# Second norm of the feed-forward part: VectorE's small operations placed between large ones, three of sixteen pairs scaled on VectorE, the output centred on GpSimd

## The reference

```python
x = _layernorm(x + self_attention(x))            # 16 heads, causal
x = _layernorm(x + cross_attention(x, ctx))      # 8 heads, rotary
h = silu(bitlinear158(x, w1, b1))                # 256 -> 1024
h = gelu(h, exact)
h = layer_norm(h, ln_g, ln_b)                    # over 1024: the second norm's input
y = bitlinear158(h, w2, b2)                      # rms_norm, rounding to 8 bits, 1024 -> 256
x = _layernorm(x + y)
```

## Time and profile before

| | us |
|---|---|
| median of 3 runs | 543.01 (540.65 to 547.83) |
| the profiled execution | 539.41 |
| its span, first to last instruction | 537.3 |
| busy in the span: PE, DVE, ACT, POOL | 428.1, 442.1, 374.3, 287.1 |

### The profile page before, as it was taken

The page is one execution under the profiler, slowest core; times in us unless marked ns, Lnnn a source line. Parts: engine busy times, 40 slices in busy tenths (PEclk is TensorE's granted clock), DMA queues, the critical chain, the costliest instruction groups (busy, mean ns, idle before and its releaser), DMA issues. The chain is left out here.

```text
span 537.3 us, 11851 instructions
## 1 busy us (share of the span) xinstructions
PE 428.1 (80%) x4098; PEld 231.1 (43%) x4098; DVE 442.1 (82%) x948; ACT 374.3 (70%) x700; POOL 287.1 (53%) x390
## 2 busy tenths in 40 slices
PE   6567799999999999999999999998876602555553
PEld 5354445445454554545545555443332201333332
DVE  3755787989889889799998998988749959999993
ACT  2232266678687786777877867677778778999983
POOL 5841646475474655645557446450124547767653
PEclk9676799999999999999999999999998855555557
DMA  6125326442332322323223232221000000000001
GB/s 226 46 77 182 93 57 187 113 114 69 82 96 63 113 70 67 108 52 111 71 64 112 66 95 69 61 89 42 3 0 1 1 0 1 11 30 20 31 30 40
DMA packets 51674, 37.07 MB, mean 69 GB/s; under 512 B 21408, under 2 KB 47648, under 8 KB 51488
## 3 DMA queue, kind: packets, MB, share of 16 engines
q1 hardware_dynamic: 51328, 36.10, 22.9%
q10 hardware_dynamic: 288, 0.23, 0.2%
HBM read 24.52 MB, written 10.49 MB: 65 GB/s over the span
## 5 line engine op out<-in xcount | busy, mean ns | idle before, releaser
L971 DVE TENSOR_REDUCE MX<-mx_b 128x2 f32<-128x512 f32 x256 | 167.1, 679 | 26.5 <-PE mx_b L581 25.4
L780 ACT ACTIVATE PB<-e_b 128x512 f32<-128x512 f32 x256 | 148.1, 592 | 55.2 <-PE e_b L609 54.0
L581 PE MATMUL mx_b<-KA,QA 48*128 48x256 bf16 x512 | 97.6, 275 | 11.5 <-DVE MX L971 10.8
L609 PE MATMUL e_b<-QA,KA 50*128 50x256 bf16 x512 | 97.1, 274 | 1.0 <-DMA QA<-MR 0.7
L626 PE MATMUL u_b<-PB,VA 128*32 128x256 f32 x1024 | 84.0, 391 | 2.0 <-ACT PB L780 1.5
L898 POOL TENSOR_TENSOR SP<-SP,srec 128x1024 f32<-128x1024 f32 x15 | 28.5, 1901 | 79.1 <-DVE srec L943 79.1
L581 PEld LDWEIGHTS mx_b<-KA,QA 48*128 48x128 bf16 x512 | 29.6, 94 | 86.7 <-issue 47.1
L1301 PE MATMUL r_b<-identh,Q 128*128 128x128 f16 x128 | 16.2, 305 | 39.5 <-ACT Q L1214 39.5
L1246 POOL TENSOR_TENSOR H<-H,row_tab 128x1024 f32<-128x1024 f32 x15 | 35.4, 2363 | 21.4 <-ACT H L1204 17.9
L1307 PE MATMUL z_b<-w2q,Q2T 128*128 128x256 bf16 x128 | 28.5, 400 | 19.3 <-ACT Q2T L1225 19.3
L888 POOL TENSOR_TENSOR KM<-QK,att_tab 128x512 f32<-128x512 f32 x31 | 32.0, 1052 | 21.4 <-ACT QK L734 21.4
(11 more groups left out here) (172 smaller groups left out, 1017.0 us busy)
## 6 DMA issues: line engine op xcount, KB each, us to landing
KA<-parts_k SPq DMA_DIRECT2D x64, 96.0 KB
QA<-parts_q SPq DMA_DIRECT2D x64, 96.0 KB
parts_q<-part_q SPq DMA_DIRECT2D x32, 128.0 KB, 1.9
parts_k<-part_k SPq DMA_DIRECT2D x16, 192.0 KB, 2.1
C<-in_ctx SPq DMA_DIRECT2D x16, 128.0 KB, 3.1
X<-in_x SPq DMA_DIRECT2D x16, 128.0 KB, 2.9
out_y<-O SPq DMA_DIRECT2D x16, 128.0 KB, 1.7
XT<-in_xT SPq DMA_DIRECT2D x15, 128.0 KB, 2.2
```

The source lines that it names most:

```text
L581: m = nc.tensor.matmul(mx_b[n % 2][:, D * k:D * k + D], QA[low:low + K_MAX, 2 * i.ring + b, h, P * u:P * u + P], KA[low:low + K_MAX, 2 * i ...
L609: m = nc.tensor.matmul(e_b[n % 2][:, D * k:D * k + D], KA[low:low + K_EXP, 2 * i.ring + b, h, P * sc:P * sc + P], QA[low:low + K_EXP, 2 * ...
L780: nc.scalar.activation(PB[:, n % 4].rearrange("p e t -> p (e t)"), e_b[n % 2][:, :], ACT.Exp, scale=XC ** -0.5).then_inc(e_sb.sem, 1)
L971: nc.vector.tensor_reduce(MX[:, b, e, 2 * q:2 * q + 2, u], mx_b[n % 2][:, :].rearrange("p (e s) -> p e s", e=2), AXL.X, ALU.max).then_inc( ...
```

## The change

- The lags are counted in VectorE's turns now (statistics 0, and so on to the output at 7), 22 turns in all. ScalarE takes gelu one pair ahead, in the same order as before.
- `shift_z` and nmz are gone: GpSimd computes O as (Z - mean) times 1/std, and waits for its own power.
- VectorE's order in a turn: base_n now stands between the shift and the inverse; the multiplier stands between the two halves of the statistics, the divisor behind them. In the first turn in which a pair gets ln_b (t == LAG_Y), this addition stands behind the statistics and not first.
- Pairs 3, 7 and 11 (VEC) are scaled on VectorE, ahead of the factors of the turn, and not on ScalarE.
- GpSimd takes the power over only as many columns as are in use in the first turns. In the drain it takes the rms's power ahead of ln_g, and writes an output in the turn of its sum.
- In turn END (19) VectorE computes the factors of the last two pairs in one turn, ScalarE rounds the last pair one turn earlier, and TensorE transposes it ahead of the product of the pair before.

```diff
@@ -1178,12 +1178,22 @@
             return Pair(0, t - lag) if 0 <= t - lag < NPAIR else None
 
 
-        LAG_G, LAG_N, LAG_Z = 1, 5, 7
+        LAG_G, LAG_Y, LAG_N, LAG_Z = 0, 3, 4, 6
         BASES = list(itertools.accumulate(sum(pair_at(t, lag) is not None for lag in (LAG_G, LAG_N, LAG_Z))
                                           for t in range(TURNS2)))
 
-        DRAIN = NPAIR + LAG_G + 1
+        DRAIN = NPAIR + LAG_G
         ROOTS = list(itertools.accumulate(1 if t < DRAIN else 2 for t in range(TURNS2)))
+        END = TURNS2 - 3
+
+        VEC = (3, 7, 11)
+        zs_vec = sem("zs_vec")
+
+        def wait_scaled(eng, i):
+            if i.v in VEC:
+                eng.wait_ge(zs_vec, sum(v <= i.v for v in VEC))
+            else:
+                eng.wait_ge(zs.sem, i.v + 1 - sum(v <= i.v for v in VEC))
 
         @block.scalar
...
             def second_values(t):
-                if i := pair_at(t, 3):
-                    wait(act, shift, i, 1)
-                    nc.scalar.activation(H[:, i.v, :], H[:, i.v, :], ACT.Identity, bias=nmh[:, i.p, 0:1],
-                                         scale=root[:, (i.v + LAG_G) % 4, 0:1]).then_inc(zs.sem, 1)
-                if i := pair_at(t, 0):
...
-                                         ACT.Identity, bias=nrnd16[:]).then_inc(q2_sb.sem, 1)
+                if t == 0:
+                    gelu_h(Pair(0, 0))
+                if (i := pair_at(t, 2)) and i.v not in VEC:
+                    scale_h(i)
+                if i := pair_at(t, -1):
+                    gelu_h(i)
+                if (j := pair_at(t, 5)) and t <= END:
+                    round_y(j)
+                if i := pair_at(t, LAG_Y):
+                    square_y(i)
+                if t == END:
+                    round_y(last)
+                if j := pair_at(t, 5):
+                    q2t_copy(j)
...
+            def power(t, col, n):
+                nc.gpsimd.tensor_tensor(root[:, t % 4, col:col + n], base[:, t % 2, col:col + n], halves[:, 0:n],
+                                        ALU.pow).then_inc(s_root, 1)
+
+            def row_product(t):
+                if i := pair_at(t, LAG_Y):
+
+                    wait(pool, yn, i, 1)
+                if (i := pair_at(t, 2)) and i.v != NPAIR - 1:
+                    wait_scaled(pool, i)
+                    nc.gpsimd.tensor_tensor(H[:, i.v, :], H[:, i.v, :], gam, ALU.mult).then_inc(zg.sem, 1)
+
+            def output(z, t):
+                pool.wait_ge(s_root, ROOTS[t])
+                if has(z, 2):
+                    pool.wait_ge(st_o[z.p], 16 * z.uses)
+                nc.gpsimd.tensor_scalar(O[:, z.p, :], Z[:, z.ring, :], mvz[:, z.p, 0:1], root[:, t % 4, 2:3],
+                                        ALU.subtract, ALU.mult).then_inc(on.sem, 1)
+
             def turn(t):
-                if i := pair_at(t, 4):
...
-                                                    ALU.pow).then_inc(s_root, 1)
-                        else:
-                            pool.sem_inc(s_root, 1)
-                elif BASES[t] > (BASES[t - 1] if t else 0):
+                if t < DRAIN:
+                    row_product(t)
+                    if z := pair_at(t, LAG_Z + 1):
+                        output(z, t - 1)
                     pool.wait_ge(s_base, BASES[t] + 1)
-                    nc.gpsimd.tensor_tensor(root[:, t % 4, :], base[:, t % 2, :], halves[:, 0:3], ALU.pow).then_inc(s_root, 1)
+                    power(t, 0, 1 + sum(t >= lag for lag in (LAG_N, LAG_Z)))
                 else:
-                    pool.sem_inc(s_root, 1)
+                    if pair_at(t, LAG_N):
+                        pool.wait_ge(s_base, BASES[t - 1] + 2)
+                        power(t, 1, 1)
+                    else:
+                        pool.sem_inc(s_root, 1)
+                    row_product(t)
+                    if t == DRAIN:
+                        output(pair_at(t, LAG_Z + 1), t - 1)
+                    pool.wait_ge(s_base, BASES[t] + 1)
+                    power(t, 2, 1)
+                    output(pair_at(t, LAG_Z), t)
 
             mean_power(pool, 1)
             rstd(pool, ln2, last, mv2, rs2)
...
@@ -1316,6 +1358,10 @@
                     x_out_proj(pe, last, g_b[1])
                 first_product(t)
             for n in range(NPAIR):
+                if n < NPAIR - 1:
+                    q2_transpose(Pair(0, n))
+                if n == NPAIR - 2:
+                    q2_transpose(last)
                 second_product(Pair(0, n))
 
...
+                    wait_scaled(dve, j)
...
+            def base_free(t):
+                if t >= 2:
+                    dve.wait_ge(s_root, ROOTS[t - 2])
 
...
+            def scale_h(i):
+                nc.vector.tensor_scalar(H[:, i.v, :], H[:, i.v, :], mvh[:, i.p, 0:1], root[:, (i.v + LAG_G) % 4, 0:1],
+                                        ALU.subtract, ALU.mult).then_inc(zs_vec, 1)
+
...
+                if has(z, 2):
+                    wait(dve, on, z.plus(-2), 1)
...
+            def y_factors(f, t):
+                prev = root[:, t % 4, :]
+                row_ceiling(f, prev)
+                row_inverse(f)
+                row_multiplier(f, prev)
+                row_divisor(f)
+
             def turn(t):
-                i, j, z = pair_at(t, LAG_G), pair_at(t, 4), pair_at(t, LAG_Z)
-                if j:
+
+                i, j, z = pair_at(t, LAG_G), pair_at(t, LAG_Y), pair_at(t, LAG_Z)
+                f, g, prev = pair_at(t, LAG_N + 1), pair_at(t, LAG_G + 1), root[:, (t - 1) % 4, :]
+                if j and t > LAG_Y:
                     row_added(j)
-                if t > LAG_G:
+                if g:
                     dve.wait_ge(s_root, ROOTS[t - 1])
-                f, g, o = pair_at(t, LAG_N + 1), pair_at(t, LAG_G + 1), pair_at(t, LAG_Z + 1)
-                prev = root[:, (t - 1) % 4, :]
+                if (n := pair_at(t, 2)) and n.v in VEC:
+                    scale_h(n)
...
                     shift_h(g, prev)
+                if s := pair_at(t, LAG_N):
+                    base_n(s, t)
...
                 if f:
-                    row_factors(f, prev)
-                if s := pair_at(t, LAG_N):
-                    base_n(s, t)
-                if i:
-                    wait(dve, gelu, i, 1)
-                    for c in range(2):
-                        nc.vector.bn_stats(sth[:, i.p, 6 * c:6 * c + 6], H[:, i.v, 512 * c:512 * c + 512]).then_inc(hn.sem, 1)
+                    row_multiplier(f, prev)
+                h_stats(i, 1)
+                if f:
+                    row_divisor(f)
+                if j and t == LAG_Y:
...
+                    row_added(j)
                 if z:
                     z_sum(z)
-                if i:
-                    wait(dve, hn, i, 2)
-                    nc.vector.bn_aggr(mvh[:, i.p, :], sth[:, i.p, :]).then_inc(hn.sem, 1)
+                h_mean(i)
                 if z:
                     z_stats(z)
-                if i:
...
+                if j := pair_at(t, LAG_Y):
                     row_added(j)
...
+                    dve.wait_ge(s_root, ROOTS[t - 1])
+                    shift_h(g, root[:, (t - 1) % 4, :])
+                if (f := pair_at(t, LAG_N + 1)) and t <= END:
+                    dve.wait_ge(s_root, ROOTS[t - 1] - int(t > DRAIN))
+                    y_factors(f, t - 1)
                 if s := pair_at(t, LAG_N):
                     base_n(s, t)
                 if j:
                     row_max_abs(j)
...
-                    z_sum(z)
-                    z_stats(z)
-                    z_base(z, t)
+                if t == END:
+                    dve.wait_ge(s_root, ROOTS[t] - 1)
+                    y_factors(last, t)
+                z = pair_at(t, LAG_Z)
+                z_sum(z)
+                z_stats(z)
+                z_base(z, t)
 
             nc.vector.memset(base[:], 1.0).then_inc(s_base, 1)
```

More of the change, by code:

```diff
@@ new lines, in scale_h, with gelu_h, round_y @@
+            def scale_h(i):
+                wait(act, shift, i, 1)
+                nc.scalar.activation(H[:, i.v, :], H[:, i.v, :], ACT.Identity, bias=nmh[:, i.p, 0:1],
+                                     scale=root[:, (i.v + LAG_G) % 4, 0:1]).then_inc(zs.sem, 1)
+            def gelu_h(i):
+                wait(act, silu, i, 1)
+                nc.scalar.activation(H[:, i.v, :], H[:, i.v, :], ACT.Gelu).then_inc(gelu.sem, 1)
+            def round_y(j):
+                wait(act, fac, j, 3)
+                if has(j, 2):
+                    wait(act, q2_ps, j.plus(-2), 1)
+                nc.scalar.activation(Q2[:, j.p, :], H[:, j.v, :], ACT.Identity, bias=rnd16[:],
+                                     scale=sc[:, j.v, 6:7]).then_inc(qd.sem, 1)
@@ new lines, in square_y, with q2t_copy @@
+            def square_y(i):
+                wait(act, yn, i, 1)
+                if has(i, 1):
+                    wait(act, sqr, i.plus(-1), 1)
```

(28 more changed lines are left out.)

75 lines of the change are left out of this document (11 added, 64 removed).

## The result

| | before | after |
|---|---|---|
| median of the runs, us | 541.94 (4 runs, one more than shown above) | 548.92 (4 runs, 547.98 to 549.24) |
| ratio | | 1.0121, 95% interval 1.0068 to 1.0174 |
| profiled execution, its span | 539.41, 537.3 | 549.14, 547.4 |
| first gelu starts, last output ends | 432.3, 534.8 | 436.3, 544.9 |
| the stage between them | 102.5 | 108.5 |

What follows compares the result with a forecast made beforehand. VectorE was taken as the bound. Late addition +1.0, first scaling +0.4, wait for Z +0.4, eight turns +0.6 and drain -1.8 gave +0.6, +0.7 by the last output: 543.7 us, range 538.5 to 547.5.

Steps and rivals of the forecast that it cites:

- nmz between power and output falls away: GpSimd at the drain's end, behind the last rounding: without nmz the output follows the power sooner, -0.4 us.
- stands behind the output of pair 12 and ends near 527.4: GpSimd's power in turn 19 of the drain; the last rounding then starts at 528.1, before at 527.67.
- Full turns: VectorE's turn falls by nmz's 0.12 us to 5.34; ScalarE's stays 5.45; three scalings add 2.0 us.
- turn 15: Turn opened by VectorE's addition at 503.06 before; forecast to start at 505.5, after +1.0, +0.4, +0.4 and +0.6.
- Drain: From turn 15 to the last output: 30.0 us instead of 31.8, -1.8; bounds -3 to -1.
- the prediction's own signs: Wrong if ordinary turns fall much over 0.12, pairs 0 and 1 add no later, or drain gains under 1 or over 3 us.
- Scaling: 128x1024 scaling on VectorE in turns 5, 9 and 13: busy 0.75 us, cost 0.66 each, bounds 0.43 to 1.22.
- Late addition in turn 3: Pair 0's addition behind shift and statistics starts at 442.55 instead of 441.24; the second addition comes 1.0 us later.
- ScalarE waiting "about 1 us": Sign for turns 9 and 13: ScalarE's rounding waits for the multiplier, so its relief of 1.13 us is not used.
- Spreading the factors: VectorE's small operations keep their distances; spreading only avoids inverse and multiplier waiting for their own input, no gain beyond.
- faster rival: ScalarE is the true bound; each scaling gives back 1.13 us, 3.4 in all: 538.8 us, chance 0.27.
- slower rival: Scalings run at the additions' rate and meet GpSimd's power, turns 5, 9, 13: +4.7 to 547.7 us, chance 0.20.

Runs made afterwards that it cites:

- e1: Changed kernel with GpSimd's output as multiply, add instead of subtract, multiply (values not the output's): stage 104.10 us, ratio 1.0011 to the kernel before.
- e2: Changed kernel with GpSimd's output as add, multiply instead of subtract, multiply (values not the output's): stage 103.37 us, one run, 547.32 us.
- e9: Changed kernel with output adding a negated mean, no VectorE scalings, turn 3's addition first, multiplier and divisor directly behind inverse and base: stage 101.98 us, ratio 0.9943.
- e5: e2's kernel with no pair scaled on VectorE (values not the output's): stage 102.10 us, ratio 0.9984 to the kernel before.
- e10: e9 with pairs 6 and 11 scaled on VectorE behind the factors: stage 102.79 us, ratio 1.0015 to the kernel before.
- e12: Changed kernel with no scaling on VectorE and turn 3's addition first, output still subtract, multiply: stage 104.90 us, ratio 0.9992 to the kernel before.
- e13: Changed kernel with GpSimd's power ahead of the output in full turns, drain order as changed: stage 106.26 us, ratio 1.0079 to the kernel before.
- e3: Changed kernel with the output in two GpSimd steps, a one-column nmz, then multiply, add: stage 105.06 us, ratio 1.0016 to the kernel before.
- e4: Kernel before with nmz and shift_z taken out and the output as subtract, multiply: stage 104.55 us, ratio 1.0029.
- e11: Changed kernel with the output as multiply, subtract (values not the output's): stage 107.84 us, one run, 545.51 us.
- e14: e12 with each output behind the next power that a factor waits for, in full turns and drain: stage 102.46 us, ratio 0.9985 to the kernel before.

## Why the prediction was wrong

It failed at one operation that the change touches and the working passed over: **the output on GpSimd.** The step took nmz out of VectorE and gave the output's new form no term: "nmz between power and output falls away" (-0.4), with the old output's 0.56 kept in the 7.16 us from the last rounding to the end, and likewise in the power that "stands behind the output of pair 12 and ends near 527.4". No row of before showed the new form, so it had to be bounded like the scaling. It measured 1.22, and from that came nearly all that was missing, the rest being the clock of a product:

- *Full turns.* The step had GpSimd far from the bound and weighed its meetings with VectorE only for the three scalings. What met was the power and the addition of ln_b. The Trainium skill ("SBUF — State Buffer", Who interferes with whom) says that a VectorE instruction with two SBUF inputs contends with a GpSimd instruction that reads SBUF; the power of 1.94 that ends 0.72 behind the addition agrees, and the prediction used that section only for the scalings, where nothing happened. Forecast for turn 15: 73.2; measured 74.60, and 73.0 with the short output. The further wait in turn 15 itself counts for the drain.
- *Drain.* Forecast 30.0 us from turn 15, measured 33.95 (108.55 - 74.60); with the short output 31.1 and 30.4 (e1, e2). What the changed kernel has more than e1 is the wait in turn 15 (0.8), the output ahead of the last pair's power (0.7), and two longer outputs at the end (1.2). The clock adds the rest, 0.1 against e1 and 0.8 against e2: it was half for both last products, and the forecast had allowed for one.

By the prediction's own signs the drain was where it would be wrong: it was to gain 1 to 3 us and lost 2.2 (33.95 against 31.8). With the short output it gains 0.7 (e1) and 1.4 (e2).

The other steps held. Turn: 5.34 forecast, 5.31 measured. Scaling: cost 0.66 forecast, 0.71 to 0.73 measured (0.81 busy against 0.75). Late addition in turn 3 and the terms up to the first rounding: 21.0 forecast, 20.93 measured. ScalarE waiting "about 1 us" for the multiplier in turns 9 and 13: 1.60 and 1.54, and 1.04 and 1.20 with the short output (e2). Spreading the factors: no gain beyond the waits that it avoids, which are 0.08 per turn (e9). Last rounding 95.8, stage 103.2: e2 has 95.98 and 103.37. That the stage agrees so closely is in part e2's clock; e1, with the same schedule, has 104.10. Losses of the change by their size: the subtraction 3.2 us by the last rounding (after against e2) and 1.2 behind it; the late addition in turn 3 1.4; the scalings 1.3.

The *faster rival* (ScalarE the true bound) fell with e5 and e10. The *slower rival* had a wait behind a GpSimd operation as its mechanism, but at the scalings; its place was wrong and its price, 0.86 against a measured wait of 0.76, nearly right. That its 547.7 is the nearest number to 548.92 is luck: the scaling cost 0.71 to 0.73 and not 1.13, and nothing met it. The chance of 0.95 for a change within 2% came true.

What stays open: why a subtraction takes GpSimd twice as long, what sets the clock of the last products, and why e12's ratio (0.9992, up to 1.0032) is lower than its stage (+2.4 us, which would be 1.0044) says; the attention part's scatter is the likeliest reason, and it was not separated.

## What to carry to other kernels

An operation whose operators change is a new operation, even with the same operands and tile: bound it or measure it. An engine with time to spare still sets the pace where its short operation that others need stands behind a long one that nobody needs; put the needed one first, as e13 did for 2.3 us of stage with a pure reordering. And relief counts only on the engine that would otherwise start later: a rounding that waits for a factor behind the moved work gains nothing.

## What was not expected of the hardware

GpSimd: 128x256 f32 with two pointer scalars took 0.56 us as multiply, add or add, multiply, and 1.22 with a subtraction in either place.

VectorE's two-tensor addition (1.22 us) and GpSimd's power over three columns, usually 0.85 to 0.89: where the power started with the addition or up to 0.56 behind it (after, e3, e4, e11, e12), it ended 0.71 to 0.73 behind the addition's end, whatever its start; 0.05 behind it took 1.89. Where it started 0.08 us or more ahead, both took their usual time. In between, 0.01 ahead, it was VectorE that took longer, 1.26 to 1.28. The same section of the Trainium skill ("SBUF — State Buffer", Who interferes with whom) calls the shared ports an exclusive lock; by that the addition should wait for a power ahead of it, and in these rows it waits 0.06 at most.

The output beside the addition goes less evenly. Started 0.06 ahead, it took 2.27 and the addition 1.28 in the changed kernel; in e9, e10 and e14 an output that started 0.03 to 0.06 ahead kept its own time and the addition took 1.58. So VectorE can be the one that waits. The starts of GpSimd's rows are rough, and no run separates these cases.
